# Small operations of two norms' moments issued in turn on VectorE

## The reference

```python
for i in range(4):
    residual = x
    q, k, v = x @ Wq[i] + bq[i], x @ Wk[i] + bk[i], x @ Wv[i] + bv[i]
    Q, K = elu(q) + 1.0, elu(k) + 1.0
    KV, Ksum = einsum('nsh,nsh->nh', K, v), sum(K, axis=1)
    Z = 1.0 / (Q * Ksum[:, None, :] + 1e-06)
    a = gelu(gelu((Q * KV[:, None, :] * Z) @ Wo[i] + bo[i]))
    x = _ln(a + residual, ln1_s[i], ln1_b[i])                 # the first norm
    f = gelu(gelu(x @ W1[i] + b1[i]) @ W2[i] + b2[i])
    x = _ln(f + x, ln2_s[i], ln2_b[i])                        # the second norm
x = _layernorm(x0 + x)                                        # norm "x"
h = gelu_exact(x @ ternary(W_fc).T)
h = layernorm(h, ln_w, ln_b)                                  # norm "g"
x = _layernorm(x + h @ ternary(W_proj).T)                     # norm "z"
```

## Time and profile before

| what | value |
|---|---|
| median of 3 runs | 504.03 us (503.8 to 504.46) |
| profiled execution | 505.61 us, its span 503.8 us |
| mean granted TensorE clock | 0.975 |
| ScalarE busy | 397.7 us (79%) |
| VectorE: line 672, statistics, x256 | 53.5 us, mean 280 ns |
| VectorE: each of the fourteen lines of moments, x32 | 5.1 to 8.3 us |
| from one down-projection of pair 0 to the next | 48.15 to 48.51 us, steps 1 to 6 |

### The profile page before, as it was taken

How to read it: one execution, slowest core, us unless ns; L and a number is a source line. 1 busy time by engine, 2 the same in 40 slices (tenths; PEclk the granted TensorE clock), 3 DMA queues, 4 the chain that set the end, 5 groups by cost and what they waited for, 6 DMA issues and landing times.

```text
span 503.8 us, 6544 instructions
## 1 busy us (share of the span) xinstructions
PE 446.4 (89%) x2052; PEld 308.2 (61%) x2052; DVE 407.8 (81%) x1378; ACT 397.7 (79%) x554; POOL 20.0 (4%) x23
## 2 busy tenths in 40 slices
PE   3767999999899989998999899989998998989990
PEld 3546556756565656565646665666546556779890
DVE  4687779896998798689878986997689997976486
ACT  1777898979897988898888989898996566849271
POOL 2400000000000000000000000000001041010000
PEclk9888999999999999999999999999999997999996
DMA  8100000000010000001000000000002011001012
GB/s 277 58 1 1 0 23 1 0 1 1 1 42 0 23 0 1 0 2 39 3 1 1 1 0 1 1 0 3 0 0 85 0 43 42 2 1 43 2 45 81
DMA packets 5217, 10.40 MB, mean 21 GB/s; under 512 B 832, under 2 KB 1856, under 8 KB 5184
## 3 DMA queue, kind: packets, MB, share of 16 engines
q1 hardware_dynamic: 5184, 9.99, 5.9%
HBM read 7.90 MB, written 2.10 MB: 20 GB/s over the span
## 4 chain that ended last, share of the span: by engine, by line
PE 65%; DVE 21%; ACT 10%; issue 2%; DMA 1%; SPq 0%; ACTq 0%; DVEq 0%
PE tile L1111 17%; PE tile L1085 9%; PE tile L1089 9%; PE tile L1086 8%; PE tile L1130 8%; PE tile L1124 5%; PE tile L1201 4%; PE tile L1190 2%; DVE xl L701 2%; DVE nt L679 2%; ACT aa L364 2%; ACT nt L379 2%; ACT x L393 2%; DVE x L689 1%; DVE stats_x L672 1%
## 5 line engine op out<-in xcount | busy, mean ns | idle before, releaser
L1085 PE MATMUL tile<-xh,wh 128*128 128x512 f32 x224 | 98.3, 439 | 21.1 <-DVE xh L270 7.8
L1111 PE MATMUL tile<-h,w 128*128 128x512 f32 x256 | 113.2, 593 | 0.1
L1086 PE MATMUL tile<-xh,wl 128*128 128x512 f32 x224 | 90.5, 404 | 0.0
L1111 PEld LDWEIGHTS tile<-h,w 128*128 128x128 f32 x256 | 47.6, 190 | 53.3 <-issue 52.4
L379 ACT ACTIVATE nt<-tile,work 128x128 f32<-128x128 f32 x176 | 64.8, 465 | 16.9 <-DVE work L666 16.9
L371 ACT ACTIVATE h<-tile,vec 128x1024 f32<-128x1024 f32 x64 | 69.2, 1116 | 9.7 <-PE tile L1089 9.4
L1089 PE MATMUL tile<-xl,wh 128*128 128x512 f32 x224 | 73.2, 408 | 0.4
L1085 PEld LDWEIGHTS tile<-xh,wh 128*128 128x128 f32 x224 | 43.0, 192 | 43.9 <-issue 17.3
L672 DVE BATCH_NORM_STATS2 stats<-tile 128x6 f32<-128x128 f32 x256 | 53.5, 280 | 2.2 <-PE tile L1130 2.2
L1130 PE MATMUL tile<-ident,nt 128*128 128x128 f32 x288 | 40.7, 284 | 13.3 <-DVE nt L679 11.6
L1089 PEld LDWEIGHTS tile<-xl,wh 128*128 128x128 f32 x224 | 42.7, 194 | 14.0 <-DVE xl L701 4.2
(11 more groups left out here) (174 smaller groups left out, 683.4 us busy)
## 6 DMA issues: line engine op xcount, KB each, us to landing
x<-x_t SPq DMA_DIRECT2D x8, 512.0 KB, 5.2
out_r<-x SPq DMA_DIRECT2D x8, 256.0 KB, 2.1
raw_u<-layers SPq DMA_DIRECT2D x4, 256.0 KB, 3.3
w<-layers SPq DMA_DIRECT2D x4, 256.0 KB, 3.5
raw_a<-layers SPq DMA_DIRECT2D x4, 192.0 KB, 2.4
wo<-layers SPq DMA_DIRECT2D x4, 64.0 KB, 4.2
fc<-fc_t SPq DMA_DIRECT2D x1, 256.0 KB, 5.3
proj<-proj_t SPq DMA_DIRECT2D x1, 256.0 KB, 5.1
```

The source lines that it names most:

```text
L1085: pe.matmul(dst, wh[:, w0:w0 + P], xh[:, part(n, p, at)], start=True, stop=False)
L1086: pe.matmul(dst, wl[:, w0:w0 + P], xh[:, part(n, p, at)], start=False, stop=False)
L1111: mm = pe.matmul(dst, w2[:, (t - 1) // 2 % 2, j * P:(j + 1) * P], h[:, p, j * PAIR + at:j * PAIR + at + BANK], start=(j == 0), stop=(j == ...
```

## The change

`moments` takes several norms. It issues the same small operations as before, but for each operation first the one of the first norm, then that of the second, and so on. `hidden_moments` becomes the case "g" of it. Two places call it with two norms:

- in each of the steps 1 to 6, `moments(("2", t, 1), ("1", t, 1))` takes the place of `moments("1", t, 1)`, behind `row_stats("1", t, 1)`. `moments("2", t, 1)`, which stood ahead of this `row_stats`, is gone from there;
- in the tail `moments(("z", 0, 1), ("g", 1, 1))` takes the place of `moments("z", 0, 1)` and `hidden_moments(3)`, which stood next to each other.

All other calls have one norm and issue what they did, in the same order, but for case "g": the scaled squares are computed ahead of the squared mean, which now waits for them. The programs of the other engines are unchanged.

```diff
-            def moments(k, t, p):
...
-                dve.wait_ge(stats_ready[k][p], call + 1)
-                dve.tensor_tensor(a, even, odd, ALU.subtract).then_inc(done, 1)
-                dve.tensor_tensor(b, even2, odd2, ALU.add).then_inc(done, 1)
-                dve.tensor_tensor(m, even, odd, ALU.add).then_inc(done, 1)
...
+            def moments(*norms):
...
+                for n in norms:
+                    k, t, p = n[:3]
+                    done, base, (rstd, shift, m, v, a, b) = work_of[n]
+                    if k == "g":
+                        at = home(k, t, p)
+                        parts = (0, 1) if len(n) == 3 else n[3:]
+                        for u in parts:
...
+                            dve.wait_ge(p_mm[p], 2 * t + u + 1)
+                            dve.tensor_copy(value(k, at, MEAN)[:, u * HALF:(u + 1) * HALF].rearrange(
+                                "p (b c) -> p b c", c=2), means).then_inc(done, 1)
...
+                        dve.wait_ge(squared[at], FT // 2 * (parts[-1] + 1))
+                        dve.tensor_scalar(b, squares[:, at, rows], 1.0 / FF, OUTER_EPS, ALU.mult, ALU.add).then_inc(done, 1)
...
+                    else:
...
+                        dve.wait_ge(stats_ready[k][p], call_of(k, t) + 1)
+                        dve.tensor_tensor(a, even, odd, ALU.subtract).then_inc(done, 1)
+                        dve.tensor_tensor(b, even2, odd2, ALU.add).then_inc(done, 1)
+                        dve.tensor_tensor(m, even, odd, ALU.add).then_inc(done, 1)
...
+                for n in norms:
+                    done, base, (rstd, shift, m, v, a, b) = work_of[n]
+                    if n[0] == "g":
+                        dve.wait_ge(done, base)
+                        dve.scalar_tensor_tensor(a, m, -1.0, m, ALU.mult, ALU.mult).then_inc(done, 1)
+                    else:
+                        dve.wait_ge(done, base - 2)
+                        dve.scalar_tensor_tensor(a, a, P / 4.0, a, ALU.mult, ALU.mult).then_inc(done, 1)
...
+            def rsqrt_of(values):
...
+                for done, base, (out, shift, m, v, f, r), scale in values:
+                    dve.wait_ge(done, base)
+                    dve.tensor_scalar(r.bitcast(I32), v.bitcast(I32), -0.5, float(0x5F3759DF), ALU.mult,
+                                      ALU.add).then_inc(done, 1)
+                for done, base, (out, shift, m, v, f, r), scale in values:
+                    dve.wait_ge(done, base + 1)
+                    dve.tensor_tensor(f, r, r, ALU.mult).then_inc(done, 1)
...
                 row_stats("2", t, 1)
                 first_sum(t, 0)
-                moments("2", t, 1)
                 row_stats("1", t, 1)
-                moments("1", t, 1)
+                moments(("2", t, 1), ("1", t, 1))
                 row_stats("1", t, 0)
-                moments("1", t, 0)
+                moments(("1", t, 0))
...
             final_stats(1)
-            moments("z", 0, 1)
-            hidden_moments(3)
+            moments(("z", 0, 1), ("g", 1, 1))
             final_sum(3, 0)
```

More of the change, by code:

```diff
@@ L625, in _ @@
         def _(dve):
[L626 to L647, removed]
@@ L649, in moments, with norm_work @@
-            def moments(k, t, p):
[L651 to L655, removed]
-                dve.wait_ge(stats_ready[k][p], call + 1)
-                dve.tensor_tensor(a, even, odd, ALU.subtract).then_inc(done, 1)
-                dve.tensor_tensor(b, even2, odd2, ALU.add).then_inc(done, 1)
-                dve.tensor_tensor(m, even, odd, ALU.add).then_inc(done, 1)
[L660 to L666, removed]
+            def norm_work(k, t, p, u=None):
+                pair, rows = home(k, t, p), slice(0, ROWS) if u is None else slice(u * HALF, (u + 1) * HALF)
+                steps = HIDDEN_STEPS if k == "g" else MOMENT_STEPS
+                base = call_of(k, t) * steps + (u or 0) * (HIDDEN_STEPS - 1)
+                return moment[k][p], base, [value(k, pair, z)[:, rows] for z in range(NCOLS)]
@@ new lines, in rsqrt_of @@
+            def rsqrt_of(values):
[4 more added lines that the diff above has]
+                for done, base, (out, shift, m, v, f, r), scale in values:
+                    dve.wait_ge(done, base + 1)
+                    dve.tensor_tensor(f, r, r, ALU.mult).then_inc(done, 1)
+                for done, base, (out, shift, m, v, f, r), scale in values:
+                    dve.wait_ge(done, base + 2)
+                    dve.scalar_tensor_tensor(f, f, -0.5 * (0.375 * scale) ** 0.2, v, ALU.mult, ALU.mult).then_inc(done, 1)
+                for done, base, (out, shift, m, v, f, r), scale in values:
+                    dve.wait_ge(done, base + 3)
+                    dve.scalar_tensor_tensor(r, f, 1.5 * (0.375 * scale) ** 0.2, r, ALU.add, ALU.mult).then_inc(done, 1)
+                for done, base, (out, shift, m, v, f, r), scale in values:
+                    dve.wait_ge(done, base + 4)
+                    dve.tensor_tensor(f, r, r, ALU.mult).then_inc(done, 1)
+                for done, base, (out, shift, m, v, f, r), scale in values:
+                    dve.wait_ge(done, base + 5)
+                    dve.tensor_tensor(f, f, v, ALU.mult).then_inc(done, 1)
+                for done, base, (out, shift, m, v, f, r), scale in values:
+                    dve.wait_ge(done, base + 6)
+                    dve.scalar_tensor_tensor(f, f, -10.0 / 3 * (0.375 * scale) ** 0.4, f, ALU.add,
+                                             ALU.mult).then_inc(done, 1)
+                for done, base, (out, shift, m, v, f, r), scale in values:
+                    dve.wait_ge(done, base + 7)
+                    dve.scalar_tensor_tensor(out, f, 5.0 * (0.375 * scale) ** 0.8, r, ALU.add, ALU.mult).then_inc(done, 1)
@@ L833, in outer_low @@
                                   ALU.subtract).then_inc(x_lo["x"][p % 2], 1)
[L835 to L851, removed]
             def final_sum(p, u):
@@ L901, in _ @@
             row_stats("1", 0, 1)
-            moments("1", 0, 1)
+            moments(("1", 0, 1))
             rows("1", 0, 1, 0)
@@ L909, in _ @@
             row_stats("1", 0, 0)
-            moments("1", 0, 0)
+            moments(("1", 0, 0))
             rows("1", 0, 0, 1)
@@ L935, in _ @@
             row_stats("2", 1, 0)
-            moments("2", 1, 0)
+            moments(("2", 1, 0))
             low("2", 1, 1)
@@ L973, in _ @@
                 row_stats("2", t, 0)
-                moments("2", t, 0)
+                moments(("2", t, 0))
                 low("2", t, 1)
@@ L996, in _ @@
             row_stats("1", 7, 0)
-            moments("1", 7, 0)
+            moments(("1", 7, 0))
             rows("1", 7, 0, 0)
-            moments("2", 7, 1)
+            moments(("2", 7, 1))
             second_sum(7, 0)
@@ L1003, in _ @@
             row_stats("2", 7, 0)
-            moments("2", 7, 0)
+            moments(("2", 7, 0))
             rows("2", 7, 0, 0)
@@ L1009, in _ @@
             row_stats("1", 7, 1)
-            moments("1", 7, 1)
+            moments(("1", 7, 1))
             rows("1", 7, 1, 1)
             row_stats("x", 0, 1)
-            moments("x", 0, 1)
+            moments(("x", 0, 1))
             low("1", 7, 1)
@@ L1027, in _ @@
             row_stats("2", 8, 1)
-            moments("2", 8, 1)
+            moments(("2", 8, 1))
             rows("2", 8, 1, 0)
@@ L1031, in _ @@
             outer_sum(3)
-            moments("x", 1, 0)
+            moments(("x", 1, 0))
             rows("x", 1, 0, 1)
@@ L1035, in _ @@
             row_stats("x", 1, 1)
-            moments("x", 1, 1)
+            moments(("x", 1, 1))
             outer_low(2)
@@ L1039, in _ @@
             outer_low(3)
-            hidden_moments(0)
+            moments(("g", 0, 0))
             final_sum(0, 0)
@@ L1044, in _ @@
             final_stats(0)
-            moments("z", 0, 0)
+            moments(("z", 0, 0))
             final_rows(0, 0)
-            hidden_moments(1)
+            moments(("g", 0, 1))
             final_sum(1, 0)
@@ L1055, in _ @@
             final_stats(3)
-            moments("z", 1, 1)
+            moments(("z", 1, 1))
             final_rows(3, 0)
-            hidden_moments(2)
+            moments(("g", 1, 0))
             final_sum(2, 0)
@@ L1061, in _ @@
             final_stats(2)
-            moments("z", 1, 0)
+            moments(("z", 1, 0))
             final_rows(2, 1)
```

30 lines of the change are left out of this document (24 added, 6 removed).

## The result

The changed kernel takes 518.91 us (median of 4 runs, 516.73 to 519.6) against 503.91 us (median of 4, 503.65 to 504.46): the ratio is 1.0297, its 95% interval 1.0268 to 1.0326. It is slower by 15 us. Its profiled execution has a span of 517.5 us against 503.8.

A forecast was written before the change was run, and what follows sets the result against it. The prediction took the bound to be a chain through TensorE and ScalarE, with 1.54 us of ScalarE slack. It added 12.8 us (loop) and 1.0 (tail), 13.8 in all, giving 517.8 us; range 515 to 529.

The forecast's parts named there:

- The price of a pair: VectorE, loop: two chains issued in turn release ScalarE at +2.71 us and VectorE at +2.68, saving 2.0 us a step.
- The move: Loop: norm 2's moments wait behind TensorE's transposes; ScalarE's norm-2 rows start 3.68 us later, gelu_down 2.14 us later.
- Slack of ScalarE: Loop, ahead of gelu_down: ScalarE's norm-2 rows can start 1.54 us later before gelu_down and the chain move.
- Six steps of 2.14: Loop, steps 1 to 6: each passes on the whole 2.14 us delay, +12.8 us in all.
- chain is rigid from 186.92 on: Later half step: every wait is relative to TensorE, which works without a pause, so the 2.14 us passes on whole.
- The tail: Kernel's end: ScalarE's late final rows delay hidden squares, TensorE waits ahead of hidden_turned(2, 1); +1.0 us, hidden-moments reordering 0.
- The clock: Rival, loop: TensorE's clock falls after closely spaced pauses, costing 1.5 or 3 us a step, 522 to 536 us; chance 0.30.
- TensorE's three pauses: Loop: instead of one 1.1 us pause, TensorE pauses for 0.95, 0.9 and 1.7 us with only transposes between.
- A clock of 0.5 inside the loop: Sign of being wrong: the profile should show PEclk 1.00 in step 3, and 0.5 nowhere in the loop.

The follow-up runs named there:

- e8: Changed kernel, but in steps 2 to 5 TensorE does the first norm's pair-1 transposes ahead of the last up-projection of the other pair; 510.87 us, ratio 1.0126.
- e1: Changed kernel, but in steps 1 to 6 the two moments are issued one after the other, not in turn; 517.32 us, ratio 1.0251 to the kernel before.
- e7: Kernel before, with five unused ScalarE copies ahead of the second norm's rows in steps 2 to 6; 506.25 us, ratio 1.0036.
- e6: Kernel before, with two unused ScalarE copies ahead of the second norm's rows in steps 2 to 6; 503.88 us, ratio 0.9995.
- e5: Pair only in the tail, as in e3, with ScalarE's final rows of pair 1 moved behind the four hidden squares of pair 2; 502.9 us, ratio 0.9985.
- e2: Changed kernel with the pair of norms only in steps 1 to 6, the tail in its old order; 515.63 us, ratio 1.0232 to the kernel before.
- e3: Changed kernel with the pair only in the tail, steps 1 to 6 in their old order; 505.23 us, ratio 1.0016 to the kernel before.
- e9: e4's order, with the last pair's hidden moments split in halves, the first issued in turn with pair 3's final-norm moments; 502.47 us, ratio 0.9972.
- e11: e9 plus a second pair: the last final norm split too, its first half in turn with the second hidden half, rows redistributed; 501.34 us, ratio 0.9948.
- e10: e9, but the first half of the hidden moments is issued behind pair 3's moments, not in turn; 503.12 us, ratio 1.0005 to the kernel before.
- e4: Changed kernel's new code with no pair at all, all moments in their old places; 504.19 us, ratio 0.9994 to the kernel before.

## Why the prediction was right

The forecast was 517.8 us, the time is 518.91, inside the range, and slower as said. Step by step:

- *The price of a pair.* Said: ScalarE at +2.71 us behind the first small operation, VectorE free at +2.68. Measured: +2.69 (183.73 less 181.04) and +2.66. The rule of the Trainium skill (VectorE: DVE Perf Modes, "Rules for kernel authors") that the drain (the emptying of the engine's pipeline behind each operation) happens regardless and only the count of operations matters, by which the prediction put the pair at 4.79, is not borne out: two pairs of operations stand 0.20 us apart, as two single ones did. The same page's "The DRAIN you can't avoid" also says that a next operation that is not held starts earlier, and with that the trace agrees: operations that wait for nothing start 0.08 us apart, though each takes 0.16.
- *The move.* Said: VectorE idle 1.8 us, rows 2 at 179.81, gelu_down at 185.41, last rows on TensorE at 189.06. Measured in step 3, less the 3.91 us of delay before it: idle 1.77, 179.82, 185.31, 189.06. e8 and e1 show that it is this wait and not the chain.
- *Slack of ScalarE.* Said 1.54 us; e7 measures 1.54.
- *Six steps of 2.14.* Said 12.8, measured 11.81 by the marks. This is the term that was mis-sized, and the step of the prediction that failed is that TensorE's "chain is rigid from 186.92 on", which holds in step 3 and not in the even steps. In the even steps VectorE takes up the next layer's weights in between (lines 713 and 715), and before the change TensorE waited for that. Timeline of the kernel before, steps 2 and 3:

```profile
138.96 1.08 PE L1130 MATMUL tile<-ident,y 128*128 128x128 f32 x8
139.26 0.69 DVE L715 TENSOR_TENSOR wl<-raw_u,wh 128x512 fp32r<-128x512 f32 x1
...
140.06 0.47 PE L1085 MATMUL tile<-xh,wh 128*128 128x512 f32 x1
...
187.42 1.07 PE L1130 MATMUL tile<-ident,y 128*128 128x128 f32 x8
188.24 0.48 PE L1085 MATMUL tile<-xh,wh 128*128 128x512 f32 x1
```

  From the transposes to the first product it takes 1.10 us in step 2 and 0.82 in step 3; the steps of the earlier trace rows's chain are 48.45 and 48.52 us long behind steps 2 and 4, 48.12 to 48.15 behind the odd ones. In step 2 VectorE's part moves by 1.0 us (line 715's counterpart starts at 142.40, less the 2.13 of step 1), TensorE's by 2.1, so afterwards the weights are there first, and from the transposes to the first product it takes 0.79 us in step 2 (143.20 to 143.99) as in step 3 (193.46 to 194.25). All steps of the changed kernel are 50.22 to 50.40 long: 2.1 us more than those behind the odd steps before, 1.8 more than those behind the even ones. Steps 2, 4 and 6 absorb 0.3 to 0.35 each, which is the 1.0 us. e6, whose steps still alternate, and e7, whose steps are all alike, show the same difference.
- *The tail.* Said +1.0, measured +1.00 (+1.1 for the pair, some -0.1 for the reordered hidden moments, which I had put at 0). The wait ahead of hidden_turned(2, 1) is there, 0.80 us, and e5 shows whose it is.
- *The clock,* a rival with 0.30. TensorE's three pauses came as said (0.94, 0.74 and 1.53 us against 0.95, 0.9 and 1.7), and the clock did fall, once in the loop, in step 5, where 1.00 was forecast. A clock of 0.5 inside the loop was one of the prediction's own signs of being wrong, so on this point it was wrong, and the time came out all the same because the fall cost little. TensorE's timeline of the changed kernel there, then one line of its table of windows (columns: window, its length, busy us of PE, PEld, DVE, ACT, POOL, each with its count, granted clock, DMA share, GB/s):

```profile
288.60 0.66 PE L1154 MATMUL tile<-ident,nt 128*128 128x128 f32 x4 [0.93 <-ACT nt L379]
289.99 2.98 PE L1154 MATMUL tile<-ident,nt 128*128 128x128 f32 x16 [0.74 <-ACT nt L379]
293.49 0.98 PE L1154 MATMUL tile<-ident,nt 128*128 128x128 f32 x4 [0.52 <-ACT nt L379]
...
290.60:294.10 3.50, 2.98 (x16) 2.58 (x15) 3.02 (x3) 3.50 (x7) 0.00 (x0) 0.52 0.00 0
```

  Sixteen transposes take 2.98 us instead of 1.97, at a mean clock of 0.52, which is 1.2 GHz. But ScalarE sets the pace there, so the next wait shrinks from 1.53 to 0.52, and this step is at most 0.18 us longer than the others (50.40 against 50.22 to 50.30). I had priced a fall at 1.5 to 3 us; the mistake was to charge it where TensorE waits anyway. It isn't always free: in e1, where the wait ahead of the last rows is only 0.34 us, TensorE's timeline at the end of step 6 has

```profile
339.38 2.56 PE L1156 MATMUL tile<-ident,nt 128*128 128x128 f32 x12 [0.96 <-DVE nt L724]
```

  and from step 6's down-projection to step 7's it takes 48.99 us, against 48.17 in the changed kernel. The clock was at 0.50 from 339.92 to 343.33. By the statement of the Trainium skill (TensorE: Matmul & The Clock Gate, Part 4) that transposes don't count as a busy TensorE the way matmuls do, such falls were likelier. The traces show one fall in the six steps of the changed kernel, one in e1, one in e2 (0.50 from 187.79 to 191.21) and none in e8, and none inside the loop in the nine profiles with the old order of the loop.
  In the tail the clock fell too, and there TensorE is on the path. Behind the same pause of 1.89 us as in the earlier trace rows, TensorE's timeline of the changed kernel has

```profile
457.26 0.73 PE L1205 MATMUL tile<-xl,tfc 128*128 128x512 f32 x2 [1.89 <-DVE xl L877]
457.83 1.81 PE L1154 MATMUL tile<-ident,nt 128*128 128x128 f32 x8
459.44 4.70 PE L1225 MATMUL tile<-pw,kq 128*128 128x129 f32 x32
```

  against 1.36 and 3.74 us before: this makes the +1.36 us of the fifth stretch. It isn't the changed code: behind the same pause (1.87 to 1.90 us) the clock stayed up in eight of the thirteen profiles, with 1.36 and 3.74 us (before, e2, e3, e5, e6, e7, e9, e11), and fell in five (the changed kernel, e1, e8, e10 and e4, which has no pair at all and takes 1.60 and 5.19 us). The stretch before it, with the low slice of the earlier trace rows, was 0.47 us shorter this time. So the span of 517.5 us, equal to the forecast's 517.6, is partly luck: 1.0 us too much in the loop, and 0.9 us (1.36 less 0.47) of clock and what else moved between the marks that was not in the sum.

The median of the runs is 1.1 us over the forecast. Run-to-run spread (516.73 to 519.6) covers it, and I don't assign it.

## What to carry to other kernels

Before giving operations a later place so that they can share a chain, look at who waits behind the result and how much slack there is: here 1.54 us of ScalarE against a delay of 3.68, read from one timeline and right to 0.1 us. Issuing two dependent chains in turn hides one of them almost whole, and is worth as much as the chain's own stretch is on the path: nothing in the loop, 2.1 us at the end of the kernel. And read every kind of step of a loop before multiplying: steps that load something extra have slack that the others lack.

## What the runs showed of the hardware

Two chains of fourteen operations each on 128x8 values, most of them dependent, take 2.66 us in turn (step 3 of the changed kernel) and 4.67 in series (e1); a half-width chain of four values for each partition (e9) is no shorter, 0.20 us from step to step. A pause of TensorE of 1.89 us left the clock up in eight profiled executions and brought it down in five, with the same instructions around it; what decides is open. A fall costs TensorE half its speed, for 3.4 us in e1's step 6, but the kernel only as far as TensorE is then what the others wait for: at most 0.2 us in step 5 of the changed kernel, 0.8 in e1's step 6, 1.4 in the tail.
